# A graph network on one core: sort with two sets of comparison banks, sweeps with half of a scaled Relu on DVE

## What is computed

```
m   = relu(ln(concat(x[dst], x[src], edge) @ W1 + b1))      # per edge, 64 wide
m   = relu(ln(m @ W2 + b2))
agg = segment_sum(m, dst)                                   # per node
x   = x + relu(ln(concat(x, agg) @ U + bu))
```

## Time and profile before

| | |
|---|---|
| median of three runs | 13711.01 us (13705.41 to 13718.18) |
| the profiled execution | 13719.76 us |
| its span, first to last instruction | 13718.0 us |
| busy: PE, DVE | 8285.5 us (60%), 6946.2 us (51%) |
| busy: ACT, POOL | 5881.8 us (43%), 6784.4 us (49%) |
| first and last scatter of the sort | 253.6 and 3104.0 us |
| first and last scaled Relu of the three sweeps | 4475.2 to 9126.6 us, with the other stages between |

### The profile page before, as it was taken

How to read it: one execution, slowest core, us unless ns; L and a number is a source line. 1 busy time by engine, 2 the same in 40 slices (tenths; PEclk the granted TensorE clock), 3 DMA queues, 4 the chain that set the end, 5 groups by cost and what they waited for, 6 DMA issues and landing times. The chain is left out here.

```text
span 13718.0 us, 359117 instructions
## 1 busy us (share of the span) xinstructions
PE 8285.5 (60%) x118615; PEld 6669.4 (49%) x118616; DVE 6946.2 (51%) x17852; ACT 5881.8 (43%) x15323; POOL 6784.4 (49%) x7062
## 2 busy tenths in 40 slices
PE   4444444444437888667776677765677745544666
PEld 3222223323336666566665666655555533433555
DVE  5444444443342777535664356653488874126331
ACT  1333333334422898526775267752277743005000
POOL 1555555555530777406774067740188832640662
PEclk9999999996559999799997999977999988559665
DMA  8010111108979666385452854437877768669773
GB/s 330 29 30 29 29 30 29 29 27 293 319 189 379 195 191 190 100 340 188 153 154 82 334 191 152 153 86 231 334 225 226 226 234 338 209 181 411 248 244 103
DMA packets 1248124, 2558.79 MB, mean 187 GB/s; under 512 B 291243, under 2 KB 630460, under 8 KB 1229246
## 3 DMA queue, kind: packets, MB, share of 16 engines
q1 hardware_dynamic: 912414, 1397.93, 31.3%
q0 software_dynamic: 232416, 575.55, 14.5%
q10 hardware_dynamic: 103104, 582.79, 10.2%
HBM read 1590.06 MB, written 965.35 MB: 186 GB/s over the span
## 5 line engine op out<-in xcount | busy, mean ns | idle before, releaser
L615 POOL DMA_INDIRECT by_src<-sort_rec,slots x1560 | 1529.3, 980 | 1560.5 <-DVE sort_rec L689 872.0
L1306 POOL DMA_INDIRECT NEAR<-spread_f,gather_ids_l x1368 | 1339.3, 979 | 459.3 <-issue 220.6
L1407 ACT ACTIVATE zr_l<-z_l,stat_l 128x64 f32<-128x64 f32 x5472 | 1372.8, 336 | 0.0
L601 ACT ACTIVATE junk<-bank,minus_one 128x384 bf16<-128x384 f32 (+1 forms) x784 | 496.9, 634 | 1339.1 <-remote 786.6
L1436 PE MATMUL bank<-NEARB,hot_t_l 128*128 x16416 | 791.1, 196 | 354.2 <-DVE z_l L1365 203.3
L735 PE MATMUL bank<-hots_t 104*128 104x128 bf16 (+3 forms) x1568 | 610.5, 464 | 605.5 <-ACT junk L601 469.4
L1436 PEld LDWEIGHTS bank<-NEARB,hot_t_l 128*128 128x128 bf16 x16416 | 659.4, 99 | 555.6 <-issue 499.2
L1315 POOL TENSOR_TENSOR rest_l<-m_l 128x512 f32<-128x512 f32 x684 | 713.4, 1043 | 303.3 <-DVE m_l L1370 268.4
L1448 PE MATMUL bank<-wm_diag,zr_t_l 128*128 128x128 f32 x5472 | 820.5, 295 | 0.0
L1302 POOL COPY gather_ids_l<-run_ids 128x8 int32 (+1 forms) x171 | 32.6, 190 | 1571.9 <-POOLq L72 1569.5
L727 PE MATMUL bank<-hots 128*49 128x49 bf16 x1568 | 147.7, 226 | 1029.0 <-ACT hots_t L584 759.2
(11 more groups left out here) (339 smaller groups left out, 27078.9 us busy)
## 6 DMA issues: line engine op xcount, KB each, us to landing
unit_hot_a<-src_hots_t SPq DMA_DIRECT2D x342, 512.0 KB, 4.9
spread_f<-unit_rows_a ACTq DMA_DIRECT2D x342, 512.0 KB, 6.7
hot_t_l<-dst_hots_t SPq DMA_DIRECT2D x456, 256.0 KB
NEAR<-dst_hots SPq DMA_DIRECT2D x456, 256.0 KB
spread_g<-gate_unit_rows ACTq DMA_DIRECT2D x114, 1024.0 KB, 11.2
spread<-sum_unit_rows ACTq DMA_DIRECT2D x114, 768.0 KB, 9.0
spread<-last_unit_rows ACTq DMA_DIRECT2D x114, 768.0 KB, 8.9
src_hots<-move_hot SPq DMA_DIRECT2D x114, 512.0 KB
```

The costliest lines, as they stand in the source:

```text
L601: act.activation(junk[:, 0:(t + 1) * P], compared(t), ACT.Relu, bias=minus_one[:], accum_out=rank[h % 2][:, 4 * u + t:4 * u + t + 1]).then ...
L615: pool.indirect_dma_start(out=by_src, out_offset=bass.IndirectOffsetOnAxis(ap=slots[h][:, j:j + 1], axis=0), in_=rec[h][:, j, :], in_offse ...
L1306: pool.indirect_dma_start(out=far_in[h % WA][:, g * GT:(g + 1) * GT, :].rearrange("p j f -> p (j f)"), out_offset=None, in_=spread_f, in_o ...
L1407: last = act.activation(zr[h % 2][:, t, :], z[h % 2][:, t, :], ACT.Relu, scale=stat[h % WA][:, 2, t:t + 1])
```

## The change

In the sort there are now two sets of three comparison banks, one per half. Their room comes from the look-ups and the counts, which had two banks each and now share one (`banks[6]`), and so the look-up of a half waits until the pick of the half before it is done. PE does its transposes in tick n for step n and everything else of a step one tick later (`part(1)`), and ACT ranks one tick later too. On PE the comparison of a half stands ahead of the counts, and DVE ranks before it grows the tables; growing waits for the half's own look-up.

In the sweeps ACT does four of the eight scaled Relus, and DVE the other four as one operation on 256 columns (`relu_v`). One eighth of `piece2` goes from POOL to DVE (`piece2_v`).

```diff
-            same = [banks[0], banks[1], banks[2]]
+            same = [banks[0:3], banks[3:6]]
-            looked = [banks[k][:, 0:4 * 2 * NW] for k in (3, 6)]
-            grown = [banks[4 + u][0:NW, 0:NW] for u in range(2)]
+            looked = banks[6][:, 0:4 * 2 * NW]
+            grown = banks[6][0:NW, 4 * 2 * NW:4 * 2 * NW + NW]
...
@@ ACT, sort: the ranks
-                        if p := part(0):
+                        if p := part(1):
...
@@ DVE, sort: grow
-                        at_least(dve, s["looked"], m - 1)
+                        dve.wait_ge(s["looked"], m)
...
@@ PE, sort: counts, comparison, look-up
-                        if p := part(0):
+                        if p := part(1):
...
-                                at_least(pe, s["ranked_v"], 2 * (m - 1))
-                                at_least(pe, s["ranked_s"], 2 * (m - 1))
+                                at_least(pe, s["ranked_v"], 2 * (m - 2))
+                                at_least(pe, s["ranked_s"], 2 * (m - 2))
...
                                 at_least(pe, s["moved"], 3 * (m - 1))
-                                at_least(pe, s["picked"], m - 2)
+                                at_least(pe, s["picked"], m - 1)
...
@@ POOL, sweep
-                            pool.tensor_tensor(piece2[h % 2][:], rest[h % 2][:], top(rest[h % 2]),
+                            pool.tensor_tensor(piece2[h % 2][:, LOW:, :], rest[h % 2][:, LOW:, :], top(rest[h % 2])[:, LOW:, :],
...
@@ DVE, sweep, behind the reciprocal of part(5); HALF = 4, LOW = 1
+                            dve.wait_ge(s["rec1"], n)
+                            at_least(dve, s["relu_turned"], n - 2)
+                            dve.scalar_tensor_tensor(out=zr[h % 2][:, HALF:, :], in0=z[h % 2][:, HALF:, :], scalar=0.0,
+                                                     in1=per_tile(stat[h % WA][:, 2, HALF:], 2 * GT - HALF, D),
+                                                     op0=ALU.max, op1=ALU.mult).then_inc(s["relu_v"], 1)
...
@@ DVE, sweep, behind the additions of part(9)
+                        if p := part(8):
+                            h, st, n, nth = p
+                            dve.wait_ge(s["rest"], n)
+                            at_least(dve, s["acc_ps"], n - 2)
+                            dve.tensor_tensor(piece2[h % 2][:, 0:LOW, :], rest[h % 2][:, 0:LOW, :],
+                                              top(rest[h % 2])[:, 0:LOW, :], ALU.subtract).then_inc(s["piece2_v"], 1)
...
@@ ACT, sweep
-                            for t in range(2 * GT):
+                            for t in range(HALF):
```

More of the change, by code:

```diff
@@ L543, in sort_edges, with compared @@
             steps = NOCT
-            def compared(t):
+            def compared(u, t):
                 bank, at, width = blocks[t]
-                return same[bank][:, at:at + width]
+                return same[u][bank][:, at:at + width]
             with nc.Block() as block:
@@ L600, in tick @@
                                 for t in (2, 3):
-                                    act.activation(junk[:, 0:(t + 1) * P], compared(t), ACT.Relu, bias=minus_one[:],
+                                    act.activation(junk[:, 0:(t + 1) * P], compared(u, t), ACT.Relu, bias=minus_one[:],
                                                    accum_out=rank[h % 2][:, 4 * u + t:4 * u + t + 1]).then_inc(s["ranked_s"], 1)
                                     act.wait_ge(s["ranked_s"], 4 * (n - 1) + 2 * u + t - 1)
-                    rolling(act, steps, WS, 0, tick)
+                    rolling(act, steps, WS, 1, tick)
                 @block.gpsimd
@@ L724, in tick @@
                                 m = 2 * (n - 1) + u + 1
[L725 to L729, removed]
-                                at_least(pe, s["ranked_v"], 2 * (m - 1))
-                                at_least(pe, s["ranked_s"], 2 * (m - 1))
                                 cols = hots_t[h % 2][:, 4 * u * P:4 * (u + 1) * P]
+                                at_least(pe, s["ranked_v"], 2 * (m - 2))
+                                at_least(pe, s["ranked_s"], 2 * (m - 2))
                                 for t in range(4):
-                                    to, width = compared(t), (t + 1) * P
+                                    to, width = compared(u, t), (t + 1) * P
                                     pe.matmul(to, lhsT=cols[:, t * P:width], rhs=cols[:, 0:width], start=True, stop=False,
@@ L740, in tick @@
                                 at_least(pe, s["moved"], 3 * (m - 1))
-                                at_least(pe, s["picked"], m - 2)
+                                at_least(pe, s["picked"], m - 1)
+                                for c in range(4):
+                                    last = pe.matmul(grown, lhsT=hots[h % 2][:, 2 * (4 * u + c), 0:NW],
+                                                     rhs=hots[h % 2][:, 2 * (4 * u + c) + 1, 0:NW], start=c == 0, stop=c == 3)
+                                last.then_inc(s["grown"], 1)
                                 for c in range(4):
                                     for q in range(2):
-                                        last = pe.matmul(looked[u][:, c * 2 * NW:(c + 1) * 2 * NW],
+                                        last = pe.matmul(looked[:, c * 2 * NW:(c + 1) * 2 * NW],
                                                          lhsT=cols[0:WB, c * P:(c + 1) * P],
@@ L748, in tick @@
                                 last.then_inc(s["looked"], 1)
-                    rolling(pe, steps, WS, 0, tick)
+                    rolling(pe, steps, WS, 1, tick)
         def keys_in_window(dve, to, keys, order_, first, groups):
@@ L1238, in mpnn_pass @@
             s = {n: sem(f"{n}_l{l}") for n in (
[L1239 to L1241 removed]
+                "key", "hot", "turned", "hot_t", "near", "z", "square1", "sum1", "root1", "rec1", "relu", "relu_v", "relu_turned",
+                "relu_t", "v_ps", "square2", "sum2", "root2", "rec2", "message", "rest", "piece2", "piece2_v", "acc_ps",
+                "acc_first", "acc_added", "ids")}
             rec_in = [sem(f"rec_in{h}_l{l}") for h in range(WB8)]
```

12 lines of the change are left out of this document (8 added, 4 removed).

## The result

The changed kernel took 13934.66 us (13933.55 to 13943.01, four runs) against 13714.6 us of before beside it (13705.41 to 13726.5): 1.0161 times as long, 95% interval 1.0144 to 1.0179. It is slower, as forecast, but by 220 us and not by 489. Its recorded execution has a span of 13932.7 us, 214.7 above that of before. Two further sets of runs gave 1.0166 (1.0146 to 1.0186) and 1.0161 (1.0144 to 1.0178).

A forecast was written before the change was run, and what follows sets the result against it. The chain through PE and DVE was taken as the limit, POOL close behind. 13,720 + 370 for the sort (377 rounded) + 120 for the sweeps gave 14,210; less 9, about 14,200 us, range 13,300 to 14,650.

The forecast's parts named there:

- POOL waits for the chain through PE and DVE: Sort: PE and DVE set the step, POOL is late by the difference; its idle time by L689 grows to some 1,240 us.
- Nothing of a step starts before T: Sort: PE starts step k only after T, losing the overlap with DVE's settling; half 0's comparison ends at T + 3.65.
- T: Sort: the end of a step's last L689 on DVE, from which the forecast counts the next step's times.
- The banks and orders cost nothing by themselves: Sort: the second banks remove a wait, the shared look-up bank's wait doesn't delay, DVE's ranks before tables cost nothing.
- The look-up of half 0 is seen at b + 9.4: Sort: this look-up, through at b + 4.1, reaches DVE at about b + 9.4, making a step of 16.55 us.
- b: Sort: the start of POOL's burst of scatters, 0.80 us after T.
- the hold: Sort: PE's results come late while POOL issues indirect DMAs, from some 3 us into a burst until its end.
- Half 1's comparison lies hidden: Sort: half 1's comparison and look-up run beside DVE's work and end before they are wanted.
- The undisturbed chain of 11.3 us: Sort: the step through PE and DVE without late results, T + 11.3, above POOL's 10.2 us.
- The sweeps at +120: Sweeps: first from 5.33 to 5.85 us a step, +119; the other two taken as 0; together +120 us.
- The block of L1331 by POOL's rest: Sweeps: DVE's new Relu waits for POOL's rest to end, then runs 0.4 us, ending 1.52 us after m.
- The first rival, PE not held: Sort: late starts come from the old order alone; 11.3 us a step, -646, total 13,190 us; chance 0.20.

The follow-up runs named there:

- e11b: Kernel before with the sort's change but PE's and ACT's step in its own tick, sweeps as before; late-result chip: 13840.55 us, ratio 1.0091.
- e4: Kernel before with the sweeps' change, but DVE's scaled Relu behind the two reductions and piece2 wholly on POOL: 13608.67 us, ratio 0.9916.
- e5: Kernel before with the sweeps' change, DVE's Relu at its first place, piece2 wholly on POOL; chip without late results: 12415.21 us, ratio 1.004.
- e6b: Changed kernel's sort with sweeps as before, each burst's eight scatters issued twice, into another table; late-result chip: 15991.05 us.
- e8b: e8's kernel again, on a chip where PE's results come late: 13530.87 us, ratio 0.9872 against the kernel before.
- e3: e1 with PE's comparison, counts and look-up ahead of the transposes, and ACT's ranks ahead of its copy: 13859.11 us, ratio 1.0098.
- e1: Kernel before with the sort's part of the change alone, sweeps as before: 13954.78 us, ratio 1.0172.
- e8: e3 with POOL issuing each half's four scatters once its slots are there; chip without late results: 12351.73 us, 0.9994 against the kernel before.
- e9: Kernel before with POOL's scatters issued by halves, nothing else; chip without late results: 12361.96 us, ratio 0.9999.

## Why the prediction was right or wrong

- **POOL waits for the chain through PE and DVE: right.** Idle by L689 rose from 872 to 1106 us (forecast 1,240). A scatter takes as long as before (median 972 and 969 ns), but bursts of 16, not rare before, no longer occur.
- **Nothing of a step starts before T: right.** The comparison came at T + 3.54 (forecast 3.65), and DVE waited 504 us for it. Taking the shift back (e11b) returned 114 of 231 us (13,955 to 13,841).
- **The banks and orders cost nothing by themselves: wrong.** e11b keeps them, without the shift, and loses 118 us (3230.6 for 3104.0 at the last scatter). Which of them costs it is open.
- **The look-up of half 0 is seen at b + 9.4: this term was mis-sized.** It came at b + 6.46, 2.94 us earlier. The interpolation between two starts of the earlier trace rows took one position of the hold for a law; that one was a single look-up, and in the changed kernel the release falls elsewhere.
- **Half 1's comparison lies hidden: wrong.** It was seen at b + 11.4, 2.15 us after DVE was free; the sign given for the forecast, a long wait for half 0 and a short one for half 1, did not come. Together -2.94 + 2.15 = -0.79 us a step, 15.76 in place of 16.55, and 195 of these are 154 us of the 377. That it fits to the hundredth is chance, since the step shown took 15.86; in the mean of all steps it is -3.5 and +2.2, and 0.4 more for half 1's look-up.
- **In sum, the hold was the term of the wrong size.** The undisturbed chain of 11.3 us was right; the hold adds 4.5 us a step to it and not 5.3, less than the 5.4 that DVE already waited in the kernel before. I had checked the reading against one step of before, 13.7 us, where the mean is 14.6 and the steps go from 10.2 to 20.0 (5 and 95% of them); those of the changed kernel go from 15.3 to 16.4.
- **The sweeps at +120: wrong by 128.** The first: from m's end to L1352's start 2.28 us (forecast 2.31), and from there to the next m's end 3.41 (forecast 3.54); the mean step 5.61, not 5.85, +69. The other two were taken as unchanged although the arithmetic itself gave less than 5.13; they gained 77 together, because the root from ACT no longer came last: DVE's wait for it fell from 1.2 us a step to nothing. I had read that wait in one step of the first sweep, where it is 0.35; in the second sweep of before it is 1.2 to 1.3.
- **The block of L1331 by POOL's rest: right in kind** (1.26 us, 0.42 alone) and shown by its removal in e4. Yet the first sweep is no faster there than before.
- **The first rival, PE not held, is true, but of the chip.** On two chips nothing was late and the sort of before ran at POOL's 10.3 us (e5). The Trainium skill's "PE and ACT never wait on anyone" ("SBUF — State Buffer", "Who interferes with whom"), a rule on access to that memory, agrees with the traces of these; on the others completion came up to 13.9 us late in the kernel before, and up to 26.8 in e6b, during POOL's indirect DMAs, which the rule does not foresee. Why the chips differ is not known from these runs.

## What to carry to other kernels

Where an engine's consumer is released by "remote" long after the recorded end, ask what another engine does in just that stretch, and lengthen it (e6b) to see the wait grow: that tells a hold from a latency. Here, where critical results fell into a neighbour's burst, cutting the burst (e8b against e3) gained more than reordering the work behind it (e3 against e1). Sum an engine's waits by what ended them, before and after, before you explain a change from one step: here the suspected hold had shrunk, and the lost overlap stood on top of the list. And before a schedule is tuned around such a wait, run the kernel before on several chips: here 10% of its time was of the chip, and e8's edit, which saved 1.3% on one kind, saved nothing on the other.

## What the runs showed of the hardware

- Two kinds of chip for the same kernel: 13,713 to 13,724 us and 12,364 to 12,366 us. Of the difference some 845 us are the sort's (2850 against 2006 us, e5, whose sort is that of before), some 180 the sweeps' (5.28 and 5.10 against 5.13 and 4.78 us a step, e9); the rest lies in other stages.
- On the late kind PE's semaphore updates arrive in a bunch: in the step shown those of the comparison, counts and look-up of half 1 stand in the trace at 1512.14, 1512.20 and 1512.30 us. The 12 matmuls of counts and look-up take 1.2 us by their rows, so they had run and only their completion was held.
- The hold lasts longer the longer POOL issues indirect DMAs without a break: at most 6.8 us with 8 in a row, 13.9 to 14.6 with up to 16, 26.8 with 16 to 32 (e6b). Results finished in the first 2.7 us of a burst came on time in 188 of 195 steps of the changed kernel.
- A granted clock of 0.50 in place of 1.00 over two thirds of the sort changed its time by 2 us in 3074.
